# Layer normalisation of the quantised stage by features: first layer on centred weights, squares added over partitions

## The chip, the cores and the metric

The kernel runs on one core of a Trainium2 chip. The metric is the device time of one execution in microseconds; three runs of the kernel before give a median of 2321.88. The engines are PE (TensorE, matmuls and transposes), VectorE (DVE), ScalarE (ACT), GpSimd (POOL) and SyncE (SP, which issues DMAs). PE writes PSUM, of which there are 8 banks of 128 x 512 fp32.

## The reference

x is 8 x 1024 x 512 fp32. Three stages follow one another, each with a residual and a layer normalisation: a delta-rule attention, the quantised MLP that this change concerns, and a low-rank MLP (the reference's second attention has no value columns, so its output is zero, and the kernel only folds the extra normalisation into a factor).

```
def _qlora_linear(x, q, scale, bias, la, lb):
    w = _dequant(q, scale)
    base = jnp.einsum('btd,od->bto', x, w) + bias
    lora = jnp.einsum('btr,or->bto', jnp.einsum('btd,rd->btr', x, la), lb)
    return base + lora
h = x
for blk in range(3):
    i0, i1 = (2 * blk, 2 * blk + 1)
    y = _qlora_linear(h, qweights[i0], scales[i0], biases[i0], lora_a[i0], lora_b[i0])
    y = _layernorm(y, ln_gamma[blk], ln_beta[blk])
    y = jax.nn.gelu(y, approximate=False)
    y = _qlora_linear(y, qweights[i1], scales[i1], biases[i1], lora_a[i1], lora_b[i1])
    h = y + h
return h
```

The stage then forms layernorm(x + h).

## The kernel before

The delta-rule stage also dequantises the six 512 x 512 weights in its last chunk and leaves them in SBUF, transposed and split into a high and a low part (`kept_W_hi`, `kept_W_lo`), so that a product of fp32 precision is three matmuls: high x high, low x high, high x low. ScalarE writes the high part of a tile of 128 rows (L720), VectorE the low part (L886).

The quantised stage has 8 steps; a step takes 128 time positions of all 8 sequences, as two streams m of 4 row tiles each (512 rows). For each stream and each of the 3 blocks b:

- `enter` (block 0 only): PE transposes x into banks `tr`, ScalarE and VectorE write `h_hi` and `h_lo`. h is kept feature-major: 4 tiles k of 128 features x 512 rows.
- `up`: the first layer, **row-major**: for each row tile r, 12 matmuls with h as the stationary and W as the moving operand (L1555 to L1557) into one of 4 banks `lin`, which ScalarE has seeded with the bias row (`seed`, L1439). VectorE takes mean and variance of each row (bn_stats L1469, bn_aggr L1471), GpSimd computes (var+eps)^-0.5 (L1396, L1398), VectorE writes the normalised rows to `quant_y` (L1484).
- `turn`: PE transposes y, 16 transposes of 128x128, into `tr` (L1572); ScalarE applies gelu with gamma and beta per feature twice, to `g_hi` (L1424) and in place in the bank (L1425), and VectorE writes `g_lo` (L1491).
- `down` (blocks 0 and 1): the second layer, feature-major, W stationary and g moving (L1582 to L1584), 12 matmuls for each of 4 feature tiles j; VectorE adds bias and h (L1500; in block 0 a second pass adds `h_lo`, L1503), ScalarE and VectorE split the new h (L1434, L1460).
- `leave` (block 2): 4 transposes of h and 12 matmuls per row tile (L1613, L1601 to L1603); VectorE adds the residual x (L1515), takes statistics and normalises in place in y (L1522), and SyncE stores y to x3 (L1365).

The same buffer `quant_y` of a stream thus holds the normalised rows of every block, the residual that SyncE loads for the leave (L1361), and the output until it is stored. The order of each engine is one list written out by hand and executed in program order: step 0 straight, steps 1 to 7 as a loop whose body is the list with the leave of stream 1 of the previous step at its front, then the rest. Engines wait on semaphores only. The two streams are interleaved so that PE works on one while the others normalise the other. SyncE loads x of the next step into `kept_x_in` after the leave (L1357).

## Time and profile before

| | us |
|---|---|
| median of 3 runs | 2321.88 |
| lowest, highest | 2321.83, 2322.88 |
| the profiled execution, its own time | 2320.67 |
| its span | 2318.7 |
| PE busy | 2266.5 (98%) |
| VectorE busy | 1537.5 (66%) |
| ScalarE busy | 1197.5 (52%) |
| GpSimd busy | 786.1 (34%) |

The quantised stage lies between about 608 and 1830 us of the span; the delta-rule stage is ahead of it, the low-rank one behind it. The span is from first to last instruction; the execution's own time adds 2 us. Matmuls overlap in PE's array, so their recorded durations (0.40 us for 128x512) are longer than the distance at which they are issued; what a matmul costs is read from the distance between starts.

### The profile page before, as it was taken

To read this page: it belongs to the slowest core of one execution; us is meant where nothing else is said; L and a number is where in the kernel's file an instruction comes from. 1 tells how busy PE (TensorE), PEld (TensorE's weight loads), DVE (VectorE), ACT (ScalarE), POOL (GpSimd) and SP (SyncE) were. 2 spreads that over 40 slices of the span, in tenths; PEclk is the share of its full clock that TensorE was granted. 3 is DMA by queue.
4 is the path that set the end of the run, shared out by engine and by line. 5 is a ranking of instruction groups with operands and counts; after the bars stand their busy time and mean duration, and the time that the engine had idled before them with its cause. 6 is when DMAs were issued, how large, how long until landed. Compare 5 with 4: busy or idle time off the path is not lost.

```text
span 2318.7 us, 37476 instructions
## 1 busy us (share of the span) xinstructions
PE 2266.5 (98%) x12223; PEld 1911.4 (82%) x12223; DVE 1537.5 (66%) x2938; ACT 1197.5 (52%) x2367; POOL 786.1 (34%) x1329
## 2 busy tenths in 40 slices
PE   7999999998899999999999999999999999999997
PEld 6999999997688888888888888888888788888886
DVE  3666666676666666757657666676676766666666
ACT  4455555555534434443443534444344577777775
POOL 2565565566211112112111121111111245555555
PEclk9999999999999999999999999999999999999999
DMA  5122221244201103002021020020211413333322
GB/s 147 56 93 97 100 84 70 100 146 124 93 1 54 56 1 110 0 18 91 0 73 36 18 91 0 18 91 0 89 52 36 164 55 109 109 109 109 109 91 73
DMA packets 101735, 166.38 MB, mean 72 GB/s; under 512 B 19664, under 2 KB 22480, under 8 KB 101520
## 3 DMA queue, kind: packets, MB, share of 16 engines
q1 hardware_dynamic: 97328, 163.69, 20.8%
q10 hardware_dynamic: 4320, 1.71, 0.3%
q8 instruction: 32, 0.52, 0.1%
q14 instruction: 55, 0.45, 0.1%
HBM read 115.05 MB, written 50.33 MB: 71 GB/s over the span
## 4 chain that ended last, share of the span: by engine, by line
PE 71%; DVE 1%; POOL 1%; issue 0%; ACT 0%; POOLq 0%; DVEq 0%
PE quant_bank L1556 7%; PE quant_bank L1555 7%; PE quant_bank L1557 7%; PE quant_bank L1945 6%; PE quant_bank L1947 6%; PE quant_bank L1946 6%; PE quant_bank L1582 5%; PE quant_bank L1583 5%; PE quant_bank L1584 5%; PE quant_bank L1572 4%; PE quant_bank L1601 3%; PE quant_bank L1603 3%; PE quant_bank L1602 3%; PE quant_bank L1544 1%; PE quant_bank L1962 1%; PE quant_bank L1613 1%
## 5 line engine op out<-in xcount | busy, mean ns | idle before, releaser
L1396 POOL TENSOR_SCALAR quant_var<-quant_mv 128x1 f32<-128x1 f32 x256 | 55.6, 217 | 1007.3 <-DVE quant_mv L1471 1007.3
L1424 ACT ACTIVATE quant_g_hi<-quant_bank,kept_beta,kept_gamma 128x512 fp32r<-128x512 f32 x192 | 150.5, 784 | 395.8 <-PE quant_bank L1572 395.8
L1555 PE MATMUL quant_bank<-kept_W_hi,quant_h_hi 128*128 128x512 f32 x768 | 306.0, 398 | 0.0
L1556 PE MATMUL quant_bank<-kept_W_lo,quant_h_hi 128*128 128x512 f32 x768 | 303.9, 396 | 0.0
L1557 PE MATMUL quant_bank<-kept_W_hi,quant_h_lo 128*128 128x512 f32 x768 | 303.6, 395 | 0.0
L1469 DVE BATCH_NORM_STATS2 quant_stats<-quant_bank 128x6 f32<-128x512 f32 x192 | 134.0, 698 | 191.0 <-PE quant_bank L1557 191.0
L1910 DVE TENSOR_TENSOR mlp_g_lo<-quant_bank,mlp_g_hi 128x512 fp32r<-128x512 f32 x256 | 176.4, 689 | 105.1 <-ACT quant_bank L1847 105.0
L1846 ACT ACTIVATE mlp_g_hi<-quant_bank,mlp_b 128x512 fp32r<-128x512 f32 x256 | 177.1, 692 | 71.4 <-PE quant_bank L1947 63.8
L1582 PE MATMUL quant_bank<-quant_g_hi,kept_W_hi 128*128 128x512 f32 x512 | 205.2, 401 | 0.0
L1583 PE MATMUL quant_bank<-quant_g_hi,kept_W_lo 128*128 128x512 f32 x512 | 202.5, 396 | 0.0
L1584 PE MATMUL quant_bank<-quant_g_lo,kept_W_hi 128*128 128x512 f32 x512 | 202.4, 395 | 0.0
L1491 DVE TENSOR_TENSOR quant_g_lo<-quant_bank,quant_g_hi 128x512 fp32r<-128x512 f32 x192 | 130.3, 689 | 99.9 <-ACT quant_bank L1425 97.7
L1439 ACT ACTIVATE quant_bank<-kept_b_all 128x512 f32<-128x512 f32 x192 | 113.3, 603 | 157.3 <-DVE quant_y L1515 85.9
L1557 PEld LDWEIGHTS quant_bank<-kept_W_hi,quant_h_lo 128*128 128x128 f32 x768 | 144.2, 188 | 35.2
L1555 PEld LDWEIGHTS quant_bank<-kept_W_hi,quant_h_hi 128*128 128x128 f32 x768 | 144.3, 188 | 34.3 <-issue 0.2
L1556 PEld LDWEIGHTS quant_bank<-kept_W_lo,quant_h_hi 128*128 128x128 f32 x768 | 144.4, 188 | 34.1
L1847 ACT ACTIVATE quant_bank<-quant_bank,mlp_b 128x512 f32<-128x512 f32 x256 | 168.2, 657 | 0.0
L1484 DVE TENSOR_SCALAR quant_y<-quant_bank,quant_mv,quant_rstd 128x512 f32<-128x512 f32 x192 | 155.5, 810 | 17.2 <-POOL quant_rstd L1398 17.1
L1398 POOL TENSOR_TENSOR quant_rstd<-quant_var,quant_minus_half 128x1 f32<-128x1 f32 x256 | 142.4, 556 | 21.4
L1434 ACT ACTIVATE quant_h_hi<-kept_x_in 128x512 fp32r<-128x512 f32 x128 | 81.9, 640 | 123.8 <-DVE kept_x_in L1503 99.8
L1425 ACT ACTIVATE quant_bank<-quant_bank,kept_beta,kept_gamma 128x512 f32<-128x512 f32 x192 | 145.2, 756 | 0.0
L1805 POOL TENSOR_SCALAR mlp_z<-mlp_z,mlp_mv,mlp_rstd 128x512 f32<-128x512 f32 x60 | 123.8, 2076 | 0.0
(283 smaller groups left out, 5863.2 us busy)
## 6 DMA issues: line engine op xcount, KB each, us to landing
delta_x_in<-L_attn_x_d SPq DMA_DIRECT2D x16, 1024.0 KB, 8.2
delta_x_res<-L_attn_x_d SPq DMA_DIRECT2D x16, 1024.0 KB, 5.5
x_d<-delta_z SPq DMA_DIRECT2D x64, 256.0 KB, 2.1
kept_x_in<-x_d SPq DMA_DIRECT2D x16, 1024.0 KB, 5.2
quant_y<-x_d SPq DMA_DIRECT2D x16, 1024.0 KB, 5.1
x_d<-quant_y SPq DMA_DIRECT2D x16, 1024.0 KB, 5.1
mlp_x_in<-x_d SPq DMA_DIRECT2D x16, 1024.0 KB, 10.3
mlp_x_res<-x_d SPq DMA_DIRECT2D x16, 1024.0 KB, 6.7
```

Source lines behind the costliest of these rows:

```text
L1424: nc.scalar.activation(g_hi[m][:, k, :], tr[k][:, :], ACT.Gelu, bias=beta[:, b, k:k + 1], scale=gamma[:, b, k:k + 1])
L1425: nc.scalar.activation(tr[k][:, :], tr[k][:, :], ACT.Gelu, bias=beta[:, b, k:k + 1], scale=gamma[:, b, k:k + 1]).then_inc(s["gelu_done"], 1)
L1484: nc.vector.tensor_scalar(y[m][:, e, :], lin_of["up", m, b, e][:, :], mv[m][:, e, 0:1], rstd[m][:, e:e + 1], ALU.subtract, ALU.mult).then_ ...
L1555: mm(out, x_hi, W_hi[2 * b][:, k, :], start=False, stop=False, skip_group_check=True)
L1556: mm(out, x_hi, W_lo[2 * b][:, k, :], start=False, stop=False, skip_group_check=True)
L1557: last = mm(out, x_lo, W_hi[2 * b][:, k, :], start=False, stop=k == KT - 1, skip_group_check=True)
L1582: mm(out, W_hi[2 * b + 1][:, k, cols], g_hi[m][:, k, :], start=k == 0, stop=False)
L1583: mm(out, W_lo[2 * b + 1][:, k, cols], g_hi[m][:, k, :], start=False, stop=False)
L1584: last = mm(out, W_hi[2 * b + 1][:, k, cols], g_lo[m][:, k, :], start=False, stop=k == KT - 1)
L1846: nc.scalar.activation(g_hi[:, at, :], p_h[at][:, :], ACT.Gelu_apprx_tanh, bias=b1[:, f:f + 1])
L1847: nc.scalar.activation(p_h[at][:, :], p_h[at][:, :], ACT.Gelu_apprx_tanh, bias=b1[:, f:f + 1]).then_inc(s_["gelu_done"], 1)
L1910: nc.vector.tensor_tensor(g_lo[:, at, :], p_h[at][:, :], as_f32(g_hi[:, at, :]), ALU.subtract).then_inc(s_["g_lo_done"], 1)
```

## The change

The first layer becomes feature-major like the second. The row mean is taken out beforehand: the preparation subtracts from each column of W, in the layers 0, 2 and 4, its mean over the 512 outputs (a first ScalarE pass accumulates it into `w_mean`, the second adds it; VectorE's low part adds it too), and a prologue does the same for the biases (`b_mean`, `b_mid`, `b_root`). So `up` yields centred values with features on partitions, in the banks `tr`, and the variance of a row is the sum of squares over partitions and over the 4 feature tiles:

- ScalarE squares each tile j into y[m] (`square`), with bias and scale 1/sqrt(512) folded in;
- VectorE adds the 4 squared tiles: `part` twice, then the last one with eps (`total`);
- PE transposes the sum, 4 transposes (`total`) into bank 7; VectorE reduces along the free axis to 128 x 4 (`spread`); GpSimd takes the power -0.5 of 128 x 4; PE transposes that, broadcast, 4 transposes (`spread`), so that the factor of each row stands along the free axis on all partitions; ScalarE copies it to `rstd_row`;
- VectorE forms (bank + b_mid) * rstd_row into y[m] (`normed`), which frees the bank; gelu and `low` read y, no `turn` is left.

The seeds, the statistics of `up` and the turn go. PE's order is rebuilt: each second layer or leave of one stream has the `total` and `spread` of the other stream between its pieces, and the last k chunk of the first two `up` tiles is issued after both. `lin` has 3 banks instead of 4. x of the next step is loaded into `x_next`, which shares its place with `h_lo`, after the last `up` of the stream, and the residual after the last `low`. `square` at block 0 waits for the store of y[m] of the step before (`x_out`).

```
@@ preparation, tile @@
+                if l % 2 == 0:
+                    n = KT * (l // 2) + j
+                    nc.scalar.activation(kept.W_raw[l // 2][:, j, :], ring_bank("tile", i)[:, :], ACT.Copy, scale=-1.0 / dim,
+                                         accum_out=w_mean[:, n:n + 1]).then_inc(w_["w_mean_done"], 1)
+                    act.wait_ge(w_["w_mean_done"], n + 1)
+                    nc.scalar.activation(kept.W_hi[l][:, j, :], ring_bank("tile", i)[:, :], ACT.Identity, bias=w_mean[:, n:n + 1]).then_inc(w_["W_hi_done"], 1)
...
@@ orders @@
+        def pe_up(m, b):
+            return several("up", m, b, ((0, 0), (1, 0), (0, 1), (1, 1), 2, 3))
+        def pe_between(what, m, b, behind, norm, entering=()):
+            n, a, late = norm
+            return (several(what, m, b, ((0, 0),), behind) + one("total", n, a, late) + several(what, m, b, ((0, 1), (1, 0)), behind) + one("spread", n, a, late)
+                    + several(what, m, b, ((1, 1), 2), behind) + list(entering) + several(what, m, b, (3,), behind))
+        def pe_order():
+            order = pe_between("leave", 0, LAST, 1, (1, LAST, 1), several("enter", 0, 0, KS)) + pe_up(0, 0)
+            order += pe_between("leave", 1, LAST, 1, (0, 0, 0), several("enter", 1, 0, KS)) + pe_up(1, 0)
+            for b in range(LAST):
+                order += pe_between("down", 0, b, 0, (1, b, 0)) + pe_up(0, b + 1)
+                order += pe_between("down", 1, b, 0, (0, b + 1, 0)) + pe_up(1, b + 1)
+        def dve_leave(m, n, a, late):
+            order = one("total", n, a, late) + one("spread", n, a, late) + several("leave", m, LAST, (0,), 1) + several("normed", n, a, KS, late)
+            order += several("leave", m, LAST, (1,), 1) + several("enter", m, 0, (0, 1, 2)) + several("leave", m, LAST, (2,), 1) + several("enter", m, 0, (3,))
+            return order + several("low", n, a, KS, late) + several("leave", m, LAST, (3,), 1)
...
@@ SyncE @@
             with sp.Fori(0, STEPS - 1) as t:
                 for m in range(STREAMS):
+                    load(t + 1, m)
                     load_residual(t, m)
                 for m in range(STREAMS):
-                    load(t + 1, m)
                     store(t, m)
...
@@ ScalarE @@
+            def square(t, m, b, j):
+                s = S[m]
+                act.wait_ge(s["lin_ps"], KT * (BLOCKS * t + b) + j + 1)
+                if b == 0 and j == 0:
+                    wait(act, s["x_out"], 16 * t)
+                nc.scalar.activation(y[m][:, j, :], tr[j][:, :], ACT.Square, bias=b_root[:, b, j:j + 1], scale=ROOT).then_inc(s["sq_done"], 1)
...
@@ VectorE @@
+            def part(t, m, b, j):
+                nc.vector.tensor_tensor(y[m][:, 0, :], y[m][:, 0, :], y[m][:, j, :], ALU.add).then_inc(s["part_done"], 1)
+            def total(t, m, b, _):
+                nc.vector.scalar_tensor_tensor(y[m][:, 0, :], y[m][:, KT - 1, :], LN_EPS / P, y[m][:, 0, :], ALU.add, ALU.add).then_inc(s["sum_done"], 1)
+            def spread(t, m, b, _):
+                nc.vector.tensor_reduce(up_var[m][:, :], by_rows, mybir.AxisListType.X, ALU.add).then_inc(s["up_var_done"], 1)
+            def normed(t, m, b, j):
+                nc.vector.scalar_tensor_tensor(y[m][:, j, :], tr[j][:, :], b_mid[:, b, j:j + 1], rstd_row[:, :], ALU.add, ALU.mult).then_inc(s["normed"], 1)
...
@@ PE @@
+                for k in ks:
+                    if j == 0:
+                        pe.wait_ge(s["h_lo_done"], KT * (BLOCKS * t + b) + k + 1)
+                    mm(tr[j][:, :], W_hi[2 * b][:, k, cols], h_hi[m][:, k, :], start=k == 0, stop=False)
+                    mm(tr[j][:, :], W_lo[2 * b][:, k, cols], h_hi[m][:, k, :], start=False, stop=False)
+                    last = mm(tr[j][:, :], W_hi[2 * b][:, k, cols], h_lo[m][:, k, :], start=False, stop=k == KT - 1)
```

VectorE at the end of the loop's body, before: the last two tiles of the leave of stream 0 (quant_y_5114) between the low halves of stream 1.

```order
L1515 TENSOR_TENSOR quant_y_5114<-quant_bank,quant_y_5114 128x512
L1469 BN_STATS quant_stats_5120<-quant_y_5114 128x6
L39 REGISTER_ALU
L1471 BN_AGGR quant_mv_5122<-quant_stats_5120 128x2
L1522 TENSOR_SCALAR quant_y_5114<-quant_y_5114,quant_mv_5122,quant_rstd_5126 128x512
L1491 TENSOR_TENSOR quant_g_lo_5119<-quant_bank,quant_g_hi_5118 128x512 x2
L1514 REGISTER_ALU
L1515 TENSOR_TENSOR quant_y_5114<-quant_bank,quant_y_5114 128x512
L1469 BN_STATS quant_stats_5120<-quant_y_5114 128x6
L39 REGISTER_ALU
L1471 BN_AGGR quant_mv_5122<-quant_stats_5120 128x2
L1522 TENSOR_SCALAR quant_y_5114<-quant_y_5114,quant_mv_5122,quant_rstd_5126 128x512 x2
```

The same leave after the change (quant_y_5144 is y of stream 0), now near the front of the body: its last tile stands behind the fourth `enter` and the four low halves of stream 1.

```order
L1512 TENSOR_TENSOR quant_h_lo_5139<-quant_bank,quant_h_hi_5138 128x512
L1550 REGISTER_ALU
L1551 TENSOR_TENSOR quant_g_lo_5149<-quant_y_5145,quant_g_hi_5148 128x512
L1550 REGISTER_ALU
L1551 TENSOR_TENSOR quant_g_lo_5149<-quant_y_5145,quant_g_hi_5148 128x512
L1550 REGISTER_ALU
L1551 TENSOR_TENSOR quant_g_lo_5149<-quant_y_5145,quant_g_hi_5148 128x512 x2
L1581 REGISTER_ALU
L1582 TENSOR_TENSOR quant_y_5144<-quant_bank,quant_y_5144 128x512
L1572 BN_STATS quant_stats_5150<-quant_y_5144 128x6
L1574 BN_AGGR quant_mv_5152<-quant_stats_5150 128x2
L1589 TENSOR_SCALAR quant_y_5144<-quant_y_5144,quant_mv_5152,quant_rstd_5156 128x512 x2
```

What moved: the leave of a stream and the next step's block 0 of the same stream now follow each other directly.

ScalarE at block 0 of a step, before: after the entering of stream 0 it only seeds banks with the bias row; it writes nothing to y.

```order
L1417 ACTIVATE quant_h_hi_5110<-quant_bank 128x512
L32 REGISTER_ALU
L1439 ACTIVATE quant_bank<-kept_b_all 128x512
L32 REGISTER_ALU
L1439 ACTIVATE quant_bank<-kept_b_all 128x512
L32 REGISTER_ALU
L1439 ACTIVATE quant_bank<-kept_b_all 128x512
L32 ISA
L1439 ACTIVATE quant_bank<-kept_b_all 128x512
```

After: behind the gelus of stream 1 (quant_y_5145) come the four squares of stream 0, whose target is y of stream 0 (quant_y_5144), then the copy of the row and the gelus that use it.

```order
L1482 ACTIVATE quant_y_5145<-quant_y_5145,kept_beta,kept_gamma 128x512
L1465 ISA
L32 REGISTER_ALU
L1468 ACTIVATE quant_y_5144<-quant_bank,quant_b_root 128x512
L1465 REGISTER_ALU
L1468 ACTIVATE quant_y_5144<-quant_bank,quant_b_root 128x512
L1465 REGISTER_ALU
L1468 ACTIVATE quant_y_5144<-quant_bank,quant_b_root 128x512
L1465 REGISTER_ALU
L1468 ACTIVATE quant_y_5144<-quant_bank,quant_b_root 128x512
L1474 REGISTER_ALU
L1475 ACTIVATE quant_rstd_row<-quant_bank 128x512
```

What moved: y is written at the end of `up` of block 0, by ScalarE, and not after the statistics, by VectorE.

## Rows read from the trace of the kernel before

**Rows 1.** The page, part 1: busy us, share of span, instructions of each engine.

```profile
PE 2266.5 (98%) x12223; PEld 1911.4 (82%) x12223; DVE 1537.5 (66%) x2938; ACT 1197.5 (52%) x2367; POOL 786.1 (34%) x1329
```

**Rows 2.** Busy time in a stretch: length, each engine (instructions), clock, DMA share, GB/s.

```profile
1000.00:1200.00 200.00, 199.82 (x962) 163.69 (x961) 131.64 (x227) 85.91 (x141) 31.99 (x84) 1.00 0.10 37
```

**Rows 3.** Timeline of PE, a turn and a leave: start, duration, engine, line, operation, count.

```profile
1017.21 0.40 PE L1582 MATMUL quant_bank<-quant_g_hi,kept_W_hi 128*128 128x512 f32 x1
...
1020.48 0.39 PE L1584 MATMUL quant_bank<-quant_g_lo,kept_W_hi 128*128 128x512 f32 x1
1020.71 1.91 PE L1572 MATMUL quant_bank<-kept_ident,quant_y 128*128 128x128 f32 x16
...
1022.70 0.40 PE L1583 MATMUL quant_bank<-quant_g_hi,kept_W_lo 128*128 128x512 f32 x1
...
1027.13 0.39 PE L1584 MATMUL quant_bank<-quant_g_lo,kept_W_hi 128*128 128x512 f32 x1
1027.36 0.60 PE L1613 MATMUL quant_bank<-kept_ident,kept_x_in 128*128 128x128 f32 x4
...
1028.04 0.40 PE L1602 MATMUL quant_bank<-kept_W_lo,quant_g_hi 128*128 128x512 f32 x1
```

**Rows 4.** Timeline of SyncE's queue: stores of x3 issued, stream 0, 0 and 1.

```profile
904.91 0.40 SPq L1365 DMA_DIRECT2D x_d<-quant_y  x1
...
1057.09 0.40 SPq L1365 DMA_DIRECT2D x_d<-quant_y  x1
...
1072.63 0.40 SPq L1365 DMA_DIRECT2D x_d<-quant_y  x1
```

**Rows 5.** DMA issues of windows 1057:1058 and 1072:1074: KB, us to landing.

```profile
x_d<-quant_y SPq DMA_DIRECT2D x1, 1024.0 KB, 5.7
...
x_d<-quant_y SPq DMA_DIRECT2D x1, 1024.0 KB, 4.2
```

**Rows 6.** Timeline of VectorE at the loop's entry (752) and at a loop's end.

```profile
752.51 0.68 DVE L1515 TENSOR_TENSOR quant_y<-quant_bank,quant_y 128x512 f32<-128x512 f32 x1
...
1050.21 0.68 DVE L1515 TENSOR_TENSOR quant_y<-quant_bank,quant_y 128x512 f32<-128x512 f32 x1
...
1052.29 1.28 DVE L1491 TENSOR_TENSOR quant_g_lo<-quant_bank,quant_g_hi 128x512 fp32r<-128x512 f32 x2
1053.49 0.68 DVE L1515 TENSOR_TENSOR quant_y<-quant_bank,quant_y 128x512 f32<-128x512 f32 x1
...
1056.52 0.55 DVE L1522 TENSOR_SCALAR quant_y<-quant_y,quant_mv,quant_rstd 128x512 f32<-128x512 f32 x1 [0.51 <-POOL quant_rstd L1398]
1060.91 0.69 DVE L1515 TENSOR_TENSOR quant_y<-quant_bank,quant_y 128x512 f32<-128x512 f32 x1 [3.85 <-issue]
```

**Rows 7.** The page, part 5: busy us, mean ns of one, idle before and its releaser.

```profile
L1424 ACT ACTIVATE quant_g_hi<-quant_bank,kept_beta,kept_gamma 128x512 fp32r<-128x512 f32 x192 | 150.5, 784 | 395.8 <-PE quant_bank L1572 395.8
...
L1439 ACT ACTIVATE quant_bank<-kept_b_all 128x512 f32<-128x512 f32 x192 | 113.3, 603 | 157.3 <-DVE quant_y L1515 85.9
...
L1398 POOL TENSOR_TENSOR quant_rstd<-quant_var,quant_minus_half 128x1 f32<-128x1 f32 x256 | 142.4, 556 | 21.4
```

**Rows 8.** Timeline of ScalarE: the stage's table load; four copies out of PSUM.

```profile
626.76 1.28 ACT L1424 ACT_TABLE_LOAD   x1
...
1063.53 2.07 ACT L1417 ACTIVATE quant_h_hi<-quant_bank 128x512 fp32r<-128x512 f32 x4 [1.29 <-PE quant_bank L1544]
```

**Rows 9.** Timeline of VectorE: the additions to h in block 1 and block 0.

```profile
1027.94 0.74 DVE L1500 SCALAR_TENSOR_TENSOR kept_x_in<-quant_bank,kept_b_col,kept_x_in 128x512 f32<-128x512 f32 x1
1028.60 1.47 DVE L1460 TENSOR_TENSOR quant_h_lo<-kept_x_in,quant_h_hi 128x512 fp32r<-128x512 f32 x2
...
1105.01 0.74 DVE L1500 SCALAR_TENSOR_TENSOR kept_x_in<-quant_bank,kept_b_col,quant_h_hi 128x512 f32<-128x512 f32 x1
1105.79 0.69 DVE L1503 TENSOR_TENSOR kept_x_in<-kept_x_in,quant_h_lo 128x512 f32<-128x512 f32 x1
```

**Rows 10.** Busy time in the first stretch of the stage; the third last column is the clock.

```profile
608.00:612.00 4.00, 4.00 (x20) 3.65 (x20) 2.58 (x4) 3.56 (x7) 0.00 (x0) 0.61 0.00 0
```

**Rows 11.** Timeline of PE in the preparation: the first transposes of the last layer.

```profile
600.77 0.66 PE L1156 MATMUL delta_p_wide<-kept_ident,delta_rows 128*128 128x128 f32 x4 [2.39 <-DVE delta_rows L880]
```

More of the change, by code:

```diff
@@ new lines, in pe_order, with act_leave @@
+        def pe_order():
[4 more added lines that the diff above has]
+                order += pe_between("down", 1, b, 0, (0, b + 1, 0)) + pe_up(1, b + 1)
+            return order
+        def act_leave(m, n, a, late):
+            return (several("square", n, a, (3,), late) + one("spread", n, a, late) + several("gelu", n, a, (0, 1), late) + several("enter", m, 0, KS) + several("gelu", n, a, (2, 3), late))
@@ L1293, in run, with pool_order @@
+        def pool_order():
+            order = one("spread", 1, LAST, 1) + several("leave", 0, LAST, range(RT), 1) + one("spread", 0, 0) + several("leave", 1, LAST, range(RT), 1)
+            for b in range(LAST):
+                order += one("spread", 1, b) + one("spread", 0, b + 1)
+            return order
         def run(eng, stages, order, closing):
@@ L1302, in run @@
                         stages[what](t - behind, m, b, i)
+            for what, m, b, i, behind in order:
+                if behind and what in stages and (what, m) != ("leave", 1):
+                    stages[what](STEPS - 1, m, b, i)
             for word in closing.split():
@@ L1525, in _ @@
             first, steps_of_mlp = mlp["vector"](dve)
-            run(dve, {"enter": enter, "up": up, "turn": turn, "down": down, "leave": leave, **first}, ORDER_DVE,
+            run(dve, {"enter": enter, "part": part, "total": total, "spread": spread, "normed": normed, "low": low, "down": down, "split": split, "leave": leave, **first}, dve_order(),
                 "leave.0 xT.0 xT.1 U1 leave.1 xT.2 xT.3 leave.2 V1.0 U2.0 P leave.3")
```

349 lines of the change are left out of this document (171 added, 178 removed).

## The prediction

> **What bounds the kernel now.** I read the busy shares first: PE 98% of the span, VectorE 66%, ScalarE 52% [rows 1]. Then the stretches: in a window inside the quantised stage PE is busy 199.8 of 200 us at full granted clock [rows 2], so the stage runs at the pace at which PE issues and every wait on PE is new time. Next PE's timeline, for what one issue costs: 14 matmuls of 128x512 take 1017.21 to 1020.48, 0.2335 us each; their recorded 0.40 us overlap [rows 3]. SyncE's stores of x3 repeat at 904.91 and 1057.09, so one of the 8 steps takes 152.18 us [rows 4]. Its 576 matmuls are 134.5 us; 160 transposes are the rest. VectorE and ScalarE cost nothing today as long as they are not late; the question is where they become late.
>
> **Terms, sum against the profiled execution (2320.67 us; span 2318.7).** I call a unit one block of one stream (6 a step, 48 in all), a phase PE's work between two ends of `up`: four second-layer or leave pieces, then four `up` pieces.
>
> (a) **PE work removed.** Before, a unit turns y with 16 transposes. The second matmul after a group of 16 starts at 1022.70, where two pitches after 1020.48 would be 1020.95: 1.75 us. A group of 4 costs 1028.04 - 1027.60 = 0.44 [rows 3]. After, a unit has two groups of 4 (`total`, `spread`). 1.75 - 0.88 = 0.87 us a unit, x48 = **-42 us**. The `up` matmuls change operands, not size; I keep 0.2335, as the second layer has this form already.
>
> (b) **The chain that replaces it.** After `up` PE needs, in order: last square (ScalarE), sum (VectorE), 4 transposes, reduction (VectorE), power (GpSimd), 4 transposes, copy (ScalarE), `normed`. Costs: matmul result 0.2 behind PE's issue; a ScalarE copy out of PSUM 0.60, a gelu with column operands 0.78 [rows 7, 8]: Square has one column operand, between them, I take 0.69; VectorE sum 0.69 to 0.75 [rows 9]. So the sum is there 1.7 us after `up`; PE covers with 9 matmuls, 2.1 us (with 4 more transposes 2.5 in a leave phase). From `total` to `spread`: transposes 0.60, a reduction of 512 columns from PSUM at one pass, like other VectorE passes 0.7, the power 0.56 with its hand-overs 0.8: 2.1 us, under 12 matmuls, 2.8. At nothing, then, but with 0.4 us of slack only; if one of the unseen operations were 0.5 us longer, each unit would pay 0.1 or more.
>
> (c) **The store of x3 now lies in the chain.** This is the largest term. `square` of block 0 writes y[m], and waits until the store of y[m] of the previous step has landed. Before, at least one `up` of the other stream lay between that store and the first write of y at block 0. After, PE does leave(m), up(m, 0) and 9 matmuls, then `total` of the same m. I lay VectorE's leave phase out from PE's `total`=0. PE: pieces to 3.7, spread, row copied at 4.9. VectorE: four `normed` at a pitch of 0.66 like other PSUM reads [rows 9], to 7.6; leave 1, 2.08 us as 1050.21 to 1052.29 [rows 6], to 9.7; it waits for the last entering transpose, 9.9; three `enter` at 0.61, leave 2 (2.09), the fourth `enter`, four `low` at 0.61: 16.9; leave 3 with its power wait, 1053.49 to 1057.07 [rows 6]: 3.6, to 20.5. SyncE issues the store 0.02 later (1057.09, [rows 4]). It lands in 5.7 us beside another load, in 4.2 alone [rows 5]. So y is free at 26.3 (stream 0, the residual load of stream 1 is issued at 17) and 24.8 (stream 1). Then squares at a pitch of 0.6 and the three dependent additions: 3.5 us, so `total` could go at 29.8 and 28.3. PE is there at 24.2 (end of `up`) + 2.5 = 26.7 and + 2.1 = 26.3. Stalls **3.1 and 2.0 us**, 7 steps each: **+35 us** (bounds 25 and 45: landing 4.2 to 6 us, pitch 0.48 to 0.66). Behind the waiting square ScalarE has the other three, the copy of the row, the gelus and the high halves; all of them are needed only after `total`, so they shift with PE and cost nothing more.
>
> (c2) **Loads moved, at nothing.** x of the next step goes to its own place as soon as the stream's last `up` is done, and is read two phases later; a load lands within 6 us [rows 5]. The residual waits for the last low half (17 in the layout) instead of the last turn; stream 1 needs it at 24.2 + 3.9, it is there at 23. SyncE issues loads, residuals, then stores, in the order in which they come due, so no store sits behind a wait that ends later. Cover: 5 us; were it gone, the residual would cost its excess once per stream and step.
>
> (d) **Loop-back.** At the loop's end VectorE stood idle 3.85 us (1057.07 to 1060.91), with nothing to wait for, while at the entry (752.51) it followed at once [rows 6]. The body goes from 226 to 199 instructions. After, the loop ends between the two additions and `total`: second addition done 1.2 us before the end of `up`, +3.85, + 0.7: PE's `total` at 3.35 instead of 2.5. 0.8 x7 = **+6 us**; 0 if the shorter body no longer pays. The Trainium skill (Runtime: NRT & Kernel Launch, Instruction fetch mechanics) says that a taken branch outside a window of two pages of 256 instructions stalls for a fetch. By that neither body would pay, and the sum would be 6 us lower; this trace contradicts it for 226 instructions, so I keep the row.
>
> (e) **Fourth piece of h in block 0.** Block 0 adds two VectorE passes per feature tile (0.78 + 0.61, [rows 9]). Laying out `dve_down` in the same way (down 0 from 1.3, row copy 4.5, down 1 to 6.6, down 2 to 10.0, down 3 to 13.4, high 3, split 3 to 14.8) PE wants h_lo 3 at 14.2. 0.7 x16 = **+11 us** (0 to 16). In block 1 there is 0.7 us a tile less: no wait.
>
> (f) **Step 0, exposed.** There the leaves are dropped, so nothing covers the chain between up(0,0) and up(1,0). From the end of up(0,0): row copied 5.0, first `normed` 5.8, table load 1.28 [rows 8] and two gelu pairs on ScalarE until 9.7, then high half, low half: up(1,0) starts at 11.0, PE's own work is 2.6: +8.4. At the start of the stage the clock fell to 0.61 of full in a 4 us window after an idle stretch [rows 10]; I add 2. **+10 us** (5 to 13).
>
> (g) **Preparation.** Twelve W tiles get a second ScalarE pass, chained by its column. In the last of them PE waits for VectorE's rows (2.39 us, [rows 11]), and those queue behind `low`, which waits for ScalarE: +1 for each such group, 2 in all (0 to 6). The bias means add seven small ScalarE instructions before the first `enter`: +2. Drain at the end: +0.5. **+4.5 us.**
>
> Sum: 2320.67 - 42 + 35 + 6 + 11 + 10 + 4.5 = 2345.2; the median is 1.2 above the profiled execution: **2346 us**, 1.0% slower.
>
> **Rivals.**
> 1. *PE-bound throughout*: (a) and (f, g) only, the chain covered, the store early enough. 2322 - 42 + 15 = 2294. For it: PE was full for 199.8 of 200 us and ScalarE has half its time free. Against: the layout of (c) has to be wrong by 3 us in both phases. 3%.
> 2. *The store does not bind, (d) to (g) do*: 2346 - 35 = 2311, faster. It needs leave 3 some 3 us earlier or a landing of 2 us; rows 5 have none. 13%.
> 3. *Only (c) binds; loop-back and (e) vanish*: the shorter body is held, and VectorE's order leaves no gap: 2346 - 17 = 2329. 17%.
> 4. *The unseen operations are long*: a Square, a reduction or an accumulation that takes 0.3 us more than assumed eats the 0.4 us of (b) in every unit and lengthens (c). It decides from 0.4 us on; 0.3 us past that is 48 x 0.3 = 14: 2361, slower still. 15%.
> That the change does not do what it says is excluded by the order of instructions: 16 transposes per unit are gone, seeds and row statistics of `up` too, and the stage has one table load as before.
>
> **How the numbers follow.** The forecast has 52% (its own range 2335 to 2357). The measurement can tell 0.2%, 4.6 us. Slower by more: forecast, rival 4 and most of rival 3, 0.80; within: 0.04; faster: rivals 1 and 2, 0.16. The range 2318 to 2366 leaves out rivals 1 and 2 and the far end of 4.
>
> **What would show it.** A step of 154 us (store to store) instead of 152.18; with rival 1 it would be 147. PE idle before `total` of block 0, about 3 and 2 us, released by VectorE's sum, with ScalarE's first square of block 0 starting just as the store lands; no such idle before `total` of blocks 1 and 2, but 0.8 once a step at the loop's end. About 0.7 us on PE before the fourth k chunk of `up` in block 1. Some 8 us of idle between 620 and 640. I am wrong if that first square starts with `up` still running, or if the idle sits before `spread`.

## The result, and the profile after

The changed kernel takes 2350.07 us (median of 4 runs, 2346.15 to 2353.40) against 2321.86 for the kernel before (4 runs, 2320.93 to 2322.88): ratio 1.0121, 95% interval 1.0103 to 1.0138. It is slower, as forecast (2346), by 28 us. The profiled execution is the shortest of the four, 2346.15 us with a span of 2344.4; against the profiled execution of before it is 25.5 us longer. The sums below are made against that pair.

First the page of the changed kernel, part 1 (the answer to [rows 1]), and two steps in the table of stretches (the answer to [rows 2]; columns: stretch, length, busy time of PE, PEld, DVE, ACT, POOL with instructions, clock, DMA share, GB/s):

```profile
PE 2249.4 (96%) x11839; PEld 1876.6 (80%) x11839; DVE 1494.6 (64%) x2746; ACT 1277.6 (54%) x2449; POOL 693.6 (30%) x993
...
883.04:1038.59 155.55, 151.16 (x690) 121.43 (x689) 96.21 (x152) 72.19 (x111) 13.03 (x22) 0.98 0.11 41
1038.59:1190.49 151.90, 148.08 (x690) 119.04 (x689) 96.21 (x152) 72.20 (x111) 13.03 (x22) 1.00 0.12 41
```

PE has 384 instructions less and is still not full: in the second step 148.08 of 151.90 us. Six steps can be read off SyncE's load of x for stream 0: 154.12, 155.55, 151.90, 152.30, 151.89 and 152.40 us. Before, the steps were 152.2 each [rows 4].

What PE waits for in the stage, from the list of waits of 590 to 1860 us (total, times, longest):

```profile
PE quant_bank L1641 <- DVE quant_y L1533: 26.2, 15, 2.6
PE quant_bank L1631 <- DVE quant_h_lo L1512: 7.1, 18, 1.1
...
PE quant_bank L1648 <- POOL quant_up_rstd L1429: 2.0, 1, 2.0
PE quant_bank L1617 <- DVE quant_y L1546: 1.5, 1, 1.5
```

L1641 is PE's transposing of `total`, L1533 VectorE's last addition. Fourteen of the fifteen waits are block 0's, two a step. Here is one, in order of time, as SyncE, ScalarE, VectorE and PE show it (timeline: start, duration, engine, line, operation; in brackets the idle time before it and what ended it):

```profile
1084.56 0.40 SPq L1398 DMA_DIRECT2D x_d<-quant_y  x1
```
```profile
1088.74 2.42 ACT L1468 ACTIVATE quant_y<-quant_bank,quant_b_root 128x512 f32<-128x512 f32 x4 [11.16 <-DMA x_d<-quant_y]
```
```profile
1090.13 1.42 DVE L1525 TENSOR_TENSOR quant_y<-quant_y 128x512 f32<-128x512 f32 x2 [5.60 <-ACT quant_y L1468]
1091.59 0.69 DVE L1533 SCALAR_TENSOR_TENSOR quant_y<-quant_y 128x512 f32<-128x512 f32 x1
```
```profile
1090.56 0.40 PE L1684 MATMUL quant_bank<-kept_W_hi,quant_g_lo 128*128 128x512 f32 x1
1092.33 0.66 PE L1641 MATMUL quant_bank<-kept_ident,quant_y 128*128 128x128 f32 x4 [1.37 <-DVE quant_y L1533]
...
1120.69 0.55 PE L1641 MATMUL quant_bank<-kept_ident,quant_y 128*128 128x128 f32 x3 [1.81 <-DVE quant_y L1533]
```

The store goes out at 1084.56; 4.18 us later ScalarE, idle for 11 us, starts its four squares at a pitch of 0.58; `total` follows 3.6 us after the landing. PE's matmuls have a pitch of 0.233, so `total` was due at 1090.79 and is 1.54 us late; in stream 1 it is 1.98 late. (The idle time in the brackets is shorter than the delay by 0.17 us, the part of the last matmul's recorded 0.40 that overlaps.)

### The profile page after: what moved, and what is told of

Same layout as the page of the kernel before. It is cut to its first block, busy times and chain, and to the rows that moved or that the text cites. A ratio compares the mean times of both kernels' runs of the same rounds, so it can differ in the third digit from the quotient of the medians.

```text
span 2344.4 us, 35695 instructions
## 1 busy us (share of the span) xinstructions
PE 2249.4 (96%) x11839; PEld 1876.6 (80%) x11839; DVE 1494.6 (64%) x2746; ACT 1277.6 (54%) x2449; POOL 693.6 (30%) x993
## 3 DMA queue, kind: packets, MB, share of 16 engines
q1 hardware_dynamic: 97328, 163.69, 20.5%
## 4 chain that ended last, share of the span: by engine, by line
PE 52%; DVE 11%; ACT 5%; DMA 3%; issue 2%; POOL 1%; DVEq 0%; POOLq 0%; ACTq 0%
PE quant_bank L2002 6%; PE quant_bank L2004 6%; PE quant_bank L2003 6%; PE quant_bank L1631 5%; PE quant_bank L1632 4%; PE quant_bank L1633 4%; PE quant_bank L1661 3%; PE quant_bank L1662 3%; PE quant_bank L1663 3%; DMA x_d<-quant_y 3%; DVE quant_g_lo L1551 2%; DVE quant_h_lo L1512 2%; PE quant_bank L1682 2%; PE quant_bank L1684 2%; PE quant_bank L1683 2%
## 5 line engine op out<-in xcount | busy, mean ns | idle before, releaser
L1631 PE MATMUL quant_bank<-quant_h_hi,kept_W_hi 128*128 128x512 f32 x768 | 308.0, 401 | 7.1 <-DVE quant_h_lo L1512 7.1
L1632 PE MATMUL quant_bank<-quant_h_hi,kept_W_lo 128*128 128x512 f32 x768 | 304.3, 396 | 0.0
L1633 PE MATMUL quant_bank<-quant_h_lo,kept_W_hi 128*128 128x512 f32 x768 | 304.2, 396 | 0.0
L1631 PEld LDWEIGHTS quant_bank<-quant_h_hi,kept_W_hi 128*128 128x128 f32 x768 | 144.6, 188 | 55.0 <-DVE quant_h_lo L1512 21.5
L1546 DVE SCALAR_TENSOR_TENSOR quant_y<-quant_bank,quant_b_mid,quant_rstd_row 128x512 f32<-128x512 f32 x192 | 139.1, 745 | 54.7 <-ACT quant_rstd_row L1475 54.7
L1633 PEld LDWEIGHTS quant_bank<-quant_h_lo,kept_W_hi 128*128 128x128 f32 x768 | 144.7, 188 | 35.0
L1632 PEld LDWEIGHTS quant_bank<-quant_h_hi,kept_W_lo 128*128 128x128 f32 x768 | 144.7, 188 | 33.4
L1481 ACT ACTIVATE quant_g_hi<-quant_y,kept_beta,kept_gamma 128x512 fp32r<-128x512 f32 x192 | 154.9, 807 | 12.3 <-DVE quant_y L1546 12.3
L1482 ACT ACTIVATE quant_y<-quant_y,kept_beta,kept_gamma 128x512 f32<-128x512 f32 x192 | 154.5, 805 | 0.0
L1551 DVE TENSOR_TENSOR quant_g_lo<-quant_y,quant_g_hi 128x512 fp32r<-128x512 f32 x192 | 127.7, 685 | 3.8
```

The costliest lines, as they stand in the source:

```text
L1481: nc.scalar.activation(g_hi[m][:, k, :], y[m][:, k, :], ACT.Gelu, bias=beta[:, b, k:k + 1], scale=gamma[:, b, k:k + 1])
L1482: nc.scalar.activation(y[m][:, k, :], y[m][:, k, :], ACT.Gelu, bias=beta[:, b, k:k + 1], scale=gamma[:, b, k:k + 1]).then_inc(s["gelu_done ...
L1551: nc.vector.tensor_tensor(g_lo[m][:, k, :], y[m][:, k, :], as_f32(g_hi[m][:, k, :]), ALU.subtract).then_inc(s["g_lo_done"], 1)
L1631: mm(tr[j][:, :], W_hi[2 * b][:, k, cols], h_hi[m][:, k, :], start=k == 0, stop=False)
L1632: mm(tr[j][:, :], W_lo[2 * b][:, k, cols], h_hi[m][:, k, :], start=False, stop=False)
L1633: last = mm(tr[j][:, :], W_hi[2 * b][:, k, cols], h_lo[m][:, k, :], start=False, stop=k == KT - 1)
```

## The experiments

### The squares in another place

```
-                if b == 0 and j == 0:
-                    wait(act, s["x_out"], 16 * t)
-                nc.scalar.activation(y[m][:, j, :], tr[j][:, :], ACT.Square, ...
+                nc.scalar.activation(sq[m][:, j, :], tr[j][:, :], ACT.Square, ...
```

`sq` lies in the place of `g_lo`; the additions, the total and PE's transposes read it there too, and `normed` of block 0 has the wait for the store.

> Edit: the squared tiles, their sums and the total are written to a tile that lies in the place of g_lo of the stream (its last reader, the second layer or leave, is ahead of `up` in PE's order), so only `normed` of block 0, not the first `square`, waits for the store of x3. Theory (the store stands in the chain): in the changed kernel's trace the starts of the 4 transposes of `total` of block 0 are late by 1.54 and 1.98 us, 3.5 us a step, 25 us in 7 steps; they vanish, since `normed` comes 5 us later than the first square did. The steps of 154.1 and 155.5 us, in which the granted clock was below 1, go to the same length as the others, another 5 to 7 us. A step is then 151.9 - 3.5 = 148.4, and the time 2350 - 25 - 7 = 2318 (2314 to 2326). Rival (squares, sum and transposes are too slow by themselves, as if a Square or the additions bound): ScalarE's wait moves from the store to PE but PE still idles a us or more before `total` of block 0; 2340 or more. Rival for the clock: its drops have nothing to do with the stalls and stay: 2325.

Measured: 2315.19 us, 10 runs; ratio to the kernel before 0.9972 (0.9963 to 0.9982). The six steps are 148.21 to 148.24 us. PE's waits in the stage are now:

```profile
PE quant_bank L1632 <- DVE quant_h_lo L1511: 7.1, 18, 1.1
...
PE quant_bank L1642 <- DVE quant_sq L1532: 1.5, 1, 1.5
```

The waits of block 0 are gone but for the one of step 0, which has no store ahead of it. So the store in the chain was the stall, and nothing else in the chain (Square, additions, reduction, power) binds in a steady step. This one edit turns the change from 1.2% slower to 0.3% faster.

### The store earlier in VectorE's order

```
-            return order + several("low", n, a, KS, late) + several("leave", m, LAST, (3,), 1)
+            return order + several("leave", m, LAST, (3,), 1) + several("low", n, a, KS, late)
```

> Edit: in VectorE's leave phase the last leave tile (2.4 us) is ahead of the four low halves, not behind them; nothing else changes. Theory (the store's place in VectorE's order sets the stall): the store of x3 is issued 2.4 us earlier after `total` of the leave phase, 18.1 in place of 20.5, lands at 22.3 if it takes 4.2 us again, and the first square starts before or at the end of `up`: both stalls (1.54 and 1.98 us) go, except for what the store lands later because the residual load of the other stream is now issued about with it (5.7 us was seen in the kernel before: 0.2 and 0.5 us left). Step 148.4 to 149.2, time 2318 to 2330. Rival (the low halves, now 2.4 us later, and the residual load behind them become late): PE waits before the second layer or leave for g_lo, and the time stays within 5 us of 2350.

Measured: 2379.36 us, ratio to the kernel before 1.0251 (1.0237 to 1.0265): 29 us slower than the changed kernel. Neither theory had this. SyncE's queue, ScalarE and PE in one step:

```profile
1089.41 0.37 SPq L1394 DMA_DIRECT2D quant_y<-x_d  x1
1089.97 0.40 SPq L1398 DMA_DIRECT2D x_d<-quant_y  x1
```
```profile
1098.41 0.69 ACT L1468 ACTIVATE quant_y<-quant_bank,quant_b_root 128x512 f32<-128x512 f32 x1 [16.12 <-DMA x_d<-quant_y]
```
```profile
1102.00 1.11 PE L1641 MATMUL quant_bank<-kept_ident,quant_y 128*128 128x128 f32 x4 [6.33 <-DVE quant_y L1533]
```

The tile was ready earlier, but SyncE executes its list in order, and there the residual load of stream 1, which waits for the low halves that had been moved back, is ahead of the store of stream 0. The store left 0.56 us behind the load, ran beside it and landed after 8.4 us, not 4.2. I had priced the residual load as a transfer that comes about together, not as an instruction that blocks the queue. Stream 1, with no such load, lost its stall (the fourteen waits became seven), so the place in VectorE's order did matter.

### The same, with SyncE's list in the order in which things come due

```
+                load(t + 1, 1)
+                store(t, 0)
+                load_residual(t, 1)
+                store(t, 1)
```

> Edit: as the run with the last leave tile ahead of the low halves, and SyncE issues the store of stream 0 ahead of the residual load of stream 1, not behind it. That run was 29 us slower than the changed kernel, with the store issued 0.56 us behind the residual load and landing 8.4 us later, and PE idle 6.3 to 7 us before `total` of stream 0 but no longer before that of stream 1. Theory (two 1 MB transfers issued together share the DMA engines; the store's place in VectorE's order was right): the store goes out 2.4 us ahead of the residual load, lands in 4.2 to 6 us, at 22.3 to 24.1 after `total` of the leave phase, in place of 24.7; the first square then starts at most 0.5 us behind its need: stalls 0 to 1 us a step, time 2318 to 2328. Rival (the transfer takes 8 us whenever a load follows it within 3 us): still 6 us of idle before `total` of stream 0, 2360 or more.

Measured: 2319.73 us, ratio 0.9988 (0.9979 to 0.9997), steps of 148.25 us. The store now leaves at 1068.84 and the load at 1071.37; the store lands after 4.5 us, and both stalls are gone. The last leave has PE wait 4.0 us once for `g_lo`, which this order makes late (1.0 in the first experiment); that is most of the 4.5 us by which it is behind the first experiment.

### The last piece of h_lo earlier in VectorE's order

```
-                            ("low", 0), ("down", 3), ("low", 1), ("split", 3), ("low", 2), ("low", 3)):
+                            ("down", 3), ("low", 0), ("split", 3), ("low", 1), ("low", 2), ("low", 3)):
```

> Edit: in VectorE's second-layer phases `down 3` is ahead of `low 0` and `split 3` ahead of `low 1`; nothing else changes. Theory (VectorE's order makes h_lo 3 late in block 0): in the changed kernel each of the two phases of block 0 loses 0.49 + 0.15 + 0.1 us before k chunks of `up`, 1.5 us a step, 12 us in 8 steps; `split 3` is done 0.6 us earlier, so the 0.49 goes: 2 x 0.5 x 8 = 8 us less, 2342, step 150.9. Rival (ScalarE's high half 3, behind two gelus, is what comes last): no change in the wait, 2350.

Measured: 2339.52 us, 10.5 less than the changed kernel; ratio to before 1.0074 (1.0061 to 1.0088). PE's waits for `quant_h_lo` fall from 18 to 2, both in step 0. The shortest steps are 150.7 us, 1.16 less than 151.90; the others, up to 153.6, have longer stalls or stretches at the slow clock, as in the changed kernel. What this edit removes was, in the changed kernel:

```profile
1134.93 0.40 PE L1633 MATMUL quant_bank<-quant_h_lo,kept_W_hi 128*128 128x512 f32 x1
1135.65 0.50 PE L1631 MATMUL quant_bank<-quant_h_hi,kept_W_hi 128*128 128x512 f32 x1 [0.33 <-DVE quant_h_lo L1512]
```

0.72 us from start to start where the pitch is 0.23.

### The centring of W left out

```
-                    nc.scalar.activation(kept.W_raw[l // 2][:, j, :], ring_bank("tile", i)[:, :], ACT.Copy, scale=-1.0 / dim, accum_out=...
-                    nc.scalar.activation(kept.W_hi[l][:, j, :], ring_bank("tile", i)[:, :], ACT.Identity, bias=w_mean[:, n:n + 1])...
+                nc.scalar.activation(kept.W_hi[l][:, j, :], ring_bank("tile", i)[:, :], ACT.Copy)...
```

> Left out: the subtraction of the column means of W in the preparation (layers 0, 2, 4), so the output is not the reference's; the prologue for the biases stays. ScalarE then makes one pass per tile as in the kernel before, VectorE its plain subtraction. Theory (the added ScalarE pass is exposed in full): ScalarE's pitch per tile of an even layer is 1.28 us instead of 0.60, 12 tiles x 0.68 = 8.2 us, and the first `enter` goes from 617.1 back to 608.9 us: 2350 - 8 = 2342. Rival 1 (as the prediction had it, 1 us in two groups, the rest being the prologue for the biases): 2 us less, 2348, and the first `enter` at 615. Rival 2 (the start is late only because of the clock): the last group of matmuls of the preparation stays late.

Measured: 2342.82 us, 7.3 less than the changed kernel. The first `enter` is at 609.45 instead of 617.12. ScalarE's passes of one W tile, in the changed kernel:

```profile
604.26 0.60 ACT L723 ACTIVATE kept_W_raw<-delta_p_wide 128x512 f32<-128x512 f32 x1 [2.16 <-PE delta_p_wide L1175]
604.75 0.19 ACT L723 ACTIVATION_READ_ACCUMULATOR kept_W_raw<-delta_p_wide 128x1 f32 x1
604.98 0.69 ACT L726 ACTIVATE kept_W_hi<-delta_p_wide,delta_w_mean 128x512 fp32r<-128x512 f32 x1
605.56 0.59 ACT L723 ACTIVATE kept_W_raw<-delta_p_pair 128x512 f32<-128x512 f32 x1
```

The next tile's first pass starts 1.30 us after this one's; in the run without centring two tiles lie 0.67 apart. Twelve times 0.63 is 7.6 us: the added pass is exposed in full. The 1.6 us that are left (609.45 against 607.87 before) stay unexplained: the prologue for the biases can't be in them, for in ScalarE's order it stands behind the point where the first `enter` starts. It holds ScalarE for 2.9 us there, and the first high half of h starts behind it; this is the changed kernel:

```profile
617.10 0.63 ACT L1448 ACTIVATE quant_y<-kept_b_all 128x512 f32<-128x512 f32 x1 [2.23 <-PEq L142]
...
620.03 2.06 ACT L1460 ACTIVATE quant_h_hi<-quant_bank 128x512 fp32r<-128x512 f32 x4
```

Before, that high half started at 608.53, 0.66 us behind the first `enter` and not 2.91.

### Both improvements together, and a third

> Edit: the two changes that helped, together: squares in the place of g_lo (2315.2 alone, 34.9 less than the changed kernel) and `down 3`, `split 3` earlier in VectorE's order (2339.5 alone, 10.5 less). Theory (the two act at different places, block 0's `total` and the fourth k chunk of `up` in block 1): they add, 2350.1 - 34.9 - 10.5 = 2304.7 (2301 to 2308), with steps of 147.0 to 147.3 us, all equal: faster than the kernel before by 0.7%. Rival (part of either gain was the granted clock, which both recover): only 2309 or so.

Measured: 2305.27 us, ratio to before 0.9929 (0.9916 to 0.9943). The gains add to within a us. Steps:

```profile
874.03:1021.09 147.06, 147.06 (x690) 119.39 (x689) 95.68 (x152) 72.75 (x111) 13.01 (x22) 1.00 0.12 43
1021.09:1168.16 147.07, 147.07 (x690) 119.35 (x689) 95.67 (x152) 72.76 (x111) 13.00 (x22) 1.00 0.12 43
```

PE is full, and a step is 5.12 us shorter than before: term (a) seen bare.

The third change is to the order of the preparation: the output projection's input comes ahead of one more W tile.

```
-... new_S.1 low.0.1 tile.0.2 O low.0.2 tile.0.3 lbT.3 low.0.3
-            ogT dequant.3.1 ...
+... new_S.1 O low.0.1 tile.0.2 low.0.2
+            ogT tile.0.3 lbT.3 low.0.3 dequant.3.1 ...
```

> Edit: as the run with both changes, and in the order of the preparation `O` is ahead of `low.0.1`, and `ogT` ahead of `tile.0.3 lbT.3 low.0.3`. In the changed kernel ScalarE's high part of the transposed attention output (577.93) stands behind three W tiles of two passes each, and PE starts the output projection at 580.11, after 2.75 us of idle; in the kernel before at 576.74. Theory (ScalarE's added passes cost where they stand ahead of that step): it comes one tile and a copy earlier, 1.3 + 0.5 us, and PE's first `enter` of the quantised stage goes 1.5 us earlier: 2305.3 - 1.5 = 2303.8 (2301.5 to 2305.5). Rival (the work is only moved: the third W tile comes later by as much, and the W layers behind it with it): 2305.3, within 1 us.

Measured: 2302.38 us (5 runs), ratio 0.9916 (0.9903 to 0.9930), the fastest of all, though its interval overlaps that of the run before. The first `enter` moved from 616.40 to 614.56, as wanted, but not by the mechanism given: the output projection starts at 579.79, where it was 579.62 without the edit. What differs is the granted clock: from 576 to 584 it was 0.50 without the edit, and the projection's matmuls start 0.43 us apart; with the edit it was 1.00, and they start 0.23 apart. Why the clock stayed up isn't shown.

### The loop's end on VectorE

Term (d) of the prediction did not appear: the changed kernel has no idle time put down to "issue" on VectorE (19.5 us, 5 times, before). Five runs asked why, each with a profile and one time. What they are read by is VectorE's timeline and the packets on the instruction queue q14, 55 before and 24 in the changed kernel. The first two were made with a count of the body that left out instructions holding only a wait or an increment (226 and 199). The edit is the same in all, with other numbers:

```
+            for n in range(60):
+                nc.vector.memset(pad[:, n:n + 1], 0.0)
```

> Edit: as the run with both changes, and 60 memsets of one column of 128 values in VectorE's program ahead of the loop of the quantised stage; the loop's body is the same 199 instructions. Counted from the start of VectorE's program the body now lies from instruction 620 to 819, in place of 560 to 759; in the kernel before, with the gap of 3.85 us at each end of the loop, from 610 to 835. Theory A (place: there is a gap when the body lies across a multiple of 256 instructions, here 768): a gap of some 3.9 us, released by nothing, on VectorE at the loop's end, between its second addition and `total`, where it now waits 1.9 us for the last square. `total` is then about 2 us late and PE idles up to 1.5 us there once a step; more instruction packets on VectorE's queue than 24. Theory B (length: 199 is short enough wherever it lies): no gap, 24 packets. The 60 memsets cost 4 us or so ahead of the first `enter`; the time itself tells little. The Trainium skill (Runtime: NRT & Kernel Launch, Instruction fetch mechanics) names blocks of 256 instructions and a window of two; taken as blocks at fixed places, read on in order, it speaks for A.

> Edit: as the run with both changes, and 190 memsets of one column ahead of the loop on VectorE and 28 inside its body (7 ahead of the first addition of each `up` of blocks 1 and 2, where VectorE waits for ScalarE 2 us and more). The body has 227 instructions, as many as in the kernel before (226), and lies from 778 to 1005, between the multiples 768 and 1024 of 256. Theory A (place): no gap at the loop's end beyond the wait for the last square, 1.9 us, 24 or so instruction packets besides those for the longer program. Theory B (length): a gap of 3.85 us at each loop's end, as in the kernel before. Steps else as in the run with both changes, since the memsets lie in idle time; 190 memsets cost some 12 us ahead of the first `enter`.

Neither had a gap; 25 and 27 packets. The second had a body of 227 by that count, as long as the 226 of before, so length as I had counted it falls, and so do blocks at multiples of 256 counted from the start of the program.

> Edit: as the run with both changes, with 80 memsets ahead of the loop and 64 inside its body on VectorE (16 ahead of the first addition of each `up` of blocks 1 and 2). The two padded runs before showed no gap at the loop's end. Their lengths were counted without instructions that only hold a wait or an increment. Counted in the compiled program, VectorE's body has 293 instructions in the kernel before (834 to 1127 of its program), 225 in the changed kernel (744 to 969), 227 from 804 in the first padded run, 255 from 962 in the second. Theory C (length by the full count, with the limit between 255 and 293): the body here has 291 (888 to 1179), so the gap is back, some 3.9 us at each loop's end, hiding the 1.9 us wait for the last square: `total` of block 2 of stream 1 is 2 us late, PE idles there 1 to 1.6 us once a step, the step is 148.5 to 149 us in place of 147.1; VectorE's queue fetches some 30 packets more than 24. Theory D (the place: the kernel before lies across two multiples of 256, given an unknown shift of 150 to 190 at the program's start): with this start the same shift puts the body across one only, so no gap. Theory E (the gap belongs to what stands there: the leave's addition, VectorE working without a wait ahead of the branch): no gap either. The Trainium skill (Runtime: NRT & Kernel Launch, Instruction fetch mechanics) gives 512 instructions in blocks of 256 to an engine like VectorE; a body under one block always fits, which is theory C.

No gap, 26 packets, step 147.07. Length falls by the full count too.

> Edit: the kernel before, with 100 memsets of one column of 128 values in VectorE's program ahead of the loop of the quantised stage; the body, 293 instructions by the full count, moves from 834..1127 to 933..1226. The padded run with a body of 291 instructions (888..1179) showed no gap at the loop's end, so length alone does not make it. Theory D (place: before, the body lay across two multiples of 256 for some constant shift at the program's start, of 150 to 190; moved by 99 it lies across one): VectorE's gap of 3.85 us at the loop's end is gone, its next addition follows at once, and the 55 instruction packets of that queue fall to some 25 to 30. Theory E (the gap belongs to what stands at the loop's end: VectorE has work without a wait on both sides of the branch, where the changed kernel waits for ScalarE): the gap stays at 3.85 us with about 55 packets. The time tells little either way, since PE is busy there in the kernel before: 2322 plus 6 us for the memsets.

The gap is gone: on VectorE the leave's addition follows its predecessor at once (1061.25, start to start 0.62, where [rows 6] has 4.39), and the queue's packets fall from 55 to 26:

```profile
1060.63 0.55 DVE L1525 TENSOR_SCALAR quant_y<-quant_y,quant_mv,quant_rstd 128x512 f32<-128x512 f32 x1 [0.79 <-POOL quant_rstd L1399]
1061.25 0.69 DVE L1518 TENSOR_TENSOR quant_y<-quant_bank,quant_y 128x512 f32<-128x512 f32 x1
```

> Edit: as the run with both changes, with 26 memsets ahead of the loop and 64 inside its body on VectorE, so that the body lies from 834 to 1125 of VectorE's program by the full count, within two instructions of where it lies in the kernel before (834 to 1127), while what stands at the loop's end is that of the changed kernel. Theory D (place): a gap of some 3.9 us between the second addition and `total` at each loop's end, about 50 packets, the step 148.5 to 149 us in place of 147.07. Theory E (what stands at the loop's end): no gap beyond the wait for the last square (1.9 us), 24 to 27 packets, a step of 147.1.

The fetches are back, 55 packets, and yet the gap is not: at the loop's end VectorE's wait is only 0.4 to 0.5 us longer than without them. The loop ends between the second addition and `total` of stream 1. The queue's row on the page, of the kernel before shifted and of this run; VectorE of this run at a loop's end; and `total` at the same place in the run with both changes, which doesn't fetch there:

```profile
q14 instruction: 26, 0.21, 0.0%
```
```profile
q14 instruction: 55, 0.45, 0.1%
```
```profile
1190.57 0.69 DVE L1529 TENSOR_TENSOR quant_sq<-quant_sq 128x512 f32<-128x512 f32 x1 [2.33 <-ACT quant_sq L1468]
1193.69 0.69 DVE L1537 SCALAR_TENSOR_TENSOR quant_sq<-quant_sq 128x512 f32<-128x512 f32 x1 [2.43 <-ACT quant_sq L1468]
```
```profile
1192.12 0.69 DVE L1532 SCALAR_TENSOR_TENSOR quant_sq<-quant_sq 128x512 f32<-128x512 f32 x1 [1.99 <-ACT quant_sq L1467]
```

The profile puts the idle time down to the last square, but in the run with both changes it is 1.99 to 2.00 us at every loop's end; here it is 2.42 to 2.53 at six of them. PE has no wait for `total` in any steady step of this run, and its step is 147.14 us against 147.07.

So two things hold. Whether the loop's end fetches depends on where the body lies in the program, in both kernels: the same 293 instructions fetch at 834 and not at 933. And where it fetches, here VectorE is idle for at most 2.5 us, nearly all of it covered by the wait for the last square, while before it was idle for 3.85 with nothing to cover it. Why it is shorter here is only argued: the DMA queues are nearly idle at that point (share 0.05 from 1190 to 1194), whereas before, a load and a store were under way (0.92 from 1057 to 1061):

```profile
1190.00:1194.00 4.00, 4.00 (x21) 3.28 (x20) 1.00 (x2) 1.23 (x2) 0.00 (x0) 1.00 0.05 16
```
```profile
1057.00:1061.00 4.00, 4.00 (x21) 3.29 (x20) 0.15 (x2) 0.00 (x0) 0.00 (x0) 1.00 0.92 346
```

The Trainium skill (Runtime: NRT & Kernel Launch, Instruction fetch mechanics) says that a taken branch stalls if its target isn't in the current window of two blocks of 256. All the programs run here agree with it, if the blocks begin 155 to 190 instructions ahead of the program's own count, so that the body of before and that of the last run lie in three blocks and the others in two; that shift is fitted to these runs, not measured by itself.

## Why the prediction was right, and where not

The sign, the size and the main mechanism came out as written. By its own terms, in us, profiled execution against profiled execution:

| term | predicted | shown | from |
|---|---|---|---|
| (a) transposes removed | -42 | -41 | step 147.07 against 152.18, x8 |
| (b) chain covered | 0 | 0 in a steady step | no wait before `spread` after step 0 |
| (c) store in the chain | +35 | +25 | 3.52 in a step of 151.90, x7 |
| (d) loop's end | +6 | 0 | no gap on VectorE |
| (e) h_lo 3 in block 0 | +11 | +9 to +12 | 1.16 a step removed; 1.48 by the starts |
| (f) step 0 exposed | +10 | +10 | below |
| (g) preparation, biases, drain | +4.5 | +12 | first `enter` +9.3; biases behind it +1; stream 0's last store to the end of the span +1.6 |
| steps longer than 151.90 | 0 | +7 | the six lengths: slow clock 4.4, longer stalls 2.4 |

The shown terms sum to 22 to 25, the two executions differ by 25.5. That the changed kernel's profiled execution came within 1 us of the forecast sum (2346.15 and 2345.2) is luck: (c) and (d) were 16 too high together, (g) and the last row 15 too low.

**(c)**, the mechanism to the letter, the size too large by 10. In the layout the store went out 20.5 us after `total` of the leave phase; measured, 1084.56 - 1064.05 = 20.51. Stream 1's stall was forecast as 2.0 and is 1.98. The step that failed is the landing in stream 0: taken as 5.7 us, since a load runs beside the store [rows 5]; it took 4.2 in four steps and 4.6 to 4.7 in three, which makes that stall 1.5 to 2.1 and not 3.1. Before, the load had been issued 3.5 us ahead of the store, now 3.3 us ahead, so the distance doesn't explain it; the load was faster too (4.7 us, 5.2 before); what explains both stays open. The experiment where load and store leave 0.56 us apart shows what sharing can cost: 8.4 us.

**(d)** failed in the step "226 to 199 instructions, so the same gap". The gap is tied to the body's place in the program, which the change moved, and where it does fetch, in the last run, VectorE is 0.4 to 0.5 us later and PE waits for nothing. In the sentence beside it I said that the trace contradicted the Trainium skill (Runtime: NRT & Kernel Launch, Instruction fetch mechanics); that was a miscount of mine. The body of before has 293 instructions, more than one block, and the later runs agree with the page.

**(e)** was right in place and near in size. The layout had 0.7 for one wait; it is 0.49 at the fourth chunk and 0.15 at an earlier one with some loss behind, 0.74 a unit.

**(f)** is right as a sum. PE in step 0:

```profile
634.52 0.66 PE L1641 MATMUL quant_bank<-kept_ident,quant_y 128*128 128x128 f32 x4 [1.50 <-DVE quant_y L1533]
637.13 0.90 PE L1648 MATMUL quant_bank<-kept_ident,quant_up_rstd 128*128 128x128 f32 x4 [1.95 <-POOL quant_up_rstd L1429]
639.51 3.67 PE L1617 MATMUL quant_bank<-kept_ident,kept_x_in 128*128 128x128 f32 x16 [1.47 <-DVE quant_y L1546]
644.24 0.80 PE L1631 MATMUL quant_bank<-quant_h_hi,kept_W_hi 128*128 128x512 f32 x1 [1.06 <-DVE quant_h_lo L1512]
```

Four waits, 6.7 us of delay from start to start, where the layout had 8.4. Behind them 16 transposes in 3.67 us (1.91 at full clock, [rows 3]) and seven matmuls 0.2 slower each, 3.2 together: the slow clock, which was put at 2. The two errors largely cancel.

**(g)** is the term that was furthest off in proportion. I looked for what the second ScalarE pass delays on PE, found two groups, and priced each at 1. The step that failed is the choice of what the pass delays: the engine that sets the pace there is ScalarE itself, with 12 tiles x 0.63 on the path. The biases, put at 2 ahead of the first `enter`, stand behind it: from there to the first matmul of `up` it takes 4.45 us where it took 2.32; but 1.1 us of slow matmuls that followed before are not there now, which leaves 1. Another 1.6 ahead of the first `enter` is unexplained.

**The clock** is a term that was missing. Granted clock in stretches of 4 us after a stall of 1.9 us in one step:

```profile
934.00:938.00 4.00, 2.10 (x12) 1.48 (x11) 2.08 (x3) 2.14 (x4) 0.00 (x0) 0.97 0.00 0
938.00:942.00 4.00, 4.00 (x15) 3.22 (x14) 2.26 (x4) 0.00 (x0) 1.63 (x3) 0.60 0.00 0
942.00:946.00 4.00, 4.00 (x23) 3.32 (x22) 2.11 (x4) 1.92 (x3) 0.13 (x1) 1.00 0.00 0
```

At 938 to 942 most of the stretch runs at the lower level, 1.2 in place of 2.4 GHz. PE had stood idle for 1.9 us just before. There are three such drops in the six steps, all in the two longest; in the others, stalls as long (1.78 to 1.89) brought none. In the runs whose stalls are gone (steps of 148.2 and 147.07) no step has one. So the drops go with the stalls, but what decides which stall brings one stays open. The two longest steps are 5.9 us over 151.90. Of this, 1.4 are longer stalls (2.64 and 1.90 us of idle time, where a step of 151.90 has 1.81 and 1.37), which leaves 4.4 for the three drops, some 1.5 us each. The longer stalls come from stores that landed later: 4.6 or 4.7 us in three of the seven steps of stream 0, and once 5.0 in stream 1.

The rivals: the second one (the store does not bind) is what the first experiment makes of the kernel: 2315 where that rival had 2311. The third (2329, loop-back and (e) vanish) was half right in its cause: the loop's end cost nothing, (e) did not vanish. The fourth, slow unseen operations: the power of 128 x 4 took 1.01 us, not 0.56, and a Square 0.69 as assumed; `spread` was still on time: in step 0, where PE had nothing else, it started 2.61 us after `total`, and elsewhere 0.44 of transposes and 12 matmuls, 3.2 us, lie between the two.

## What to carry to other kernels

When an intermediate moves into a buffer that is also an output, look for the first write of the next round, not the last read: the store's landing joins the chain, and another home for the scratch values (here a tile whose last reader was already done) is worth more than any reordering. Before moving an instruction on one engine, list what the DMA queue's own order hangs on it: a load that waits longer also holds back the store behind it, and the two then share the engines. A pass added to the engine that sets the pace of a phase costs its full length times its count, whatever PE seems to wait for there.

## What was not expected of the hardware

A store of 1 MB took 4.2 us alone (once 5.0), 4.2 to 4.7 issued 3.3 us behind a load of the same size, but 5.7 to 6.0 behind one by 3.5 us in the kernel before; 0.56 us behind one it took 8.4. A loop's end on VectorE fetched instructions again (55 against 26 packets) or not, depending on where the same body stood in the program; 99 instructions of shift took away a gap of 3.85 us. A stall of PE of 1.9 us was followed, in some steps and not in others with equal stalls, by a stretch at the lower clock that cost some 1.5 us more.
